# Spreading the last two batches' first norm over the fill of a quantised feed-forward

## What is computed

```python
x = x + xattn0(layernorm(x), ctx)      # softmax attention, 16 heads
x = x + ffn0(layernorm(x))             # quantised feed-forward
x = x + xattn1(layernorm(x), ctx)      # gated mLSTM attention, 8 heads
x = x + ffn1(layernorm(x))             # linear plus gated LoRA

def ffn0(x):                           # 256 -> 1024 -> 256
    h = layernorm(x) * ln1_g + ln1_b
    h = bitlinear(h, w1, b1)           # per-token 8-bit levels, ternary weights
    h = layernorm(gelu(h)) * ln2_g + ln2_b
    return bitlinear(h, w2, b2)
```

## Time and profile before

| | us |
|---|---|
| median of 3 runs | 406.5 (406.21 to 407.29) |
| time of the profiled execution | 406.27 |
| its span | 404.6 |
| busy: PE, DVE, ACT, POOL | 332.8, 305.9, 264.3, 183.8 |

### The profile page before, as it was taken

How to read it: one execution, slowest core, us unless ns; L and a number is a source line. 1 busy time by engine, 2 the same in 40 slices (tenths; PEclk the granted TensorE clock), 3 DMA queues, 4 the chain that set the end, 5 groups by cost and what they waited for, 6 DMA issues and landing times.

```text
span 404.6 us, 9204 instructions
## 1 busy us (share of the span) xinstructions
PE 332.8 (82%) x3118; PEld 235.1 (58%) x3118; DVE 305.9 (76%) x1025; ACT 264.3 (65%) x567; POOL 183.8 (45%) x207
## 2 busy tenths in 40 slices
PE   2989789999999999922667877869887999999975
PEld 1767567776777777611444555546455666666642
DVE  2799746777898989677899899897346787778772
ACT  1566444466545545734878988988667888888732
POOL 1213500211212375228999899885105545554550
PEclk9999999999999999965899999989999999999999
DMA  7699998969553440000000000000001212221101
GB/s 238 214 291 270 251 253 224 253 137 269 119 122 81 122 62 3 1 0 0 2 1 2 0 2 1 2 0 0 2 12 29 41 42 40 54 53 42 26 27 39
DMA packets 43869, 33.68 MB, mean 83 GB/s; under 512 B 19888, under 2 KB 39728, under 8 KB 43696
## 3 DMA queue, kind: packets, MB, share of 16 engines
q1 hardware_dynamic: 43824, 33.11, 32.9%
HBM read 24.71 MB, written 8.39 MB: 82 GB/s over the span
## 4 chain that ended last, share of the span: by engine, by line
PE 53%; DVE 19%; issue 14%; ACT 8%; POOL 5%; DMA 1%; SPq 0%; POOLq 0%; DVEq 0%; ACTq 0%
PE PS L1250 5%; PE PS L1169 5%; PE PS L1486 4%; PE PS L1239 4%; DVE sm L745 4%; PE PS L1308 4%; PE PS L1472 4%; PE PS L1230 4%; PE PS L1229 4%; PE PS L1269 3%; PE PS L1445 2%; PE PS L1467 2%; ACT pT L1000 2%; DVE sm L717 2%; PE PS L1435 2%
## 5 line engine op out<-in xcount | busy, mean ns | idle before, releaser
L1000 ACT ACTIVATE pT<-PS 128x512 f32<-128x512 f32 x64 | 36.5, 596 | 48.3 <-PE PS L1230 47.9
L610 DVE TENSOR_REDUCE negm<-PS 128x4 bf16<-128x512 f32 x64 | 42.3, 684 | 13.0 <-PE PS L1239 12.8
L439 POOL TENSOR_TENSOR sm<-sm,mhalf 128x1 f32<-128x1 f32 x16 | 11.3, 708 | 81.1 <-DVE sm L642 81.1
L455 POOL TENSOR_TENSOR kst<-kst,rows 128x1024 f32<-128x1024 f32 x16 | 37.6, 2352 | 6.4 <-ACT kst L1068 6.2
L1115 ACT ACTIVATE lnT<-PS,Atok 128x128 f32<-128x128 f32 x128 | 36.3, 369 | 2.0 <-DVE lnb L853 0.8
L1348 PE MATMUL PS<-identf,w2f 128*128 128x128 f32 x128 | 19.2, 298 | 21.4 <-ACT w2f L1057 21.3
L1230 PE MATMUL PS<-identb,negm 128*128 128x128 bf16 x256 | 34.9, 220 | 0.0
L469 POOL TENSOR_TENSOR kst<-kst,rows 128x1024 f32<-128x1024 f32 x14 | 33.1, 2363 | 0.0
L1250 PE MATMUL PS<-pT,vx 128*32 128x128 f32 x512 | 27.1, 285 | 5.2 <-ACT pT L1000 5.2
L1348 PEld LDWEIGHTS PS<-identf,w2f 128*128 128x128 f32 x128 | 15.1, 151 | 26.0 <-ACT w2f L1057 20.6
L494 POOL TENSOR_TENSOR rr<-ms,mhalf 128x8 f32<-128x8 f32 x16 | 26.4, 1647 | 1.9 <-DVE ms L935 1.9
(11 more groups left out here) (222 smaller groups left out, 979.1 us busy)
## 6 DMA issues: line engine op xcount, KB each, us to landing
scr_q<-qpart SPq DMA_DIRECT2D x8, 384.0 KB, 3.3
scr_k<-kpart SPq DMA_DIRECT2D x8, 384.0 KB, 4.5
X<-in_x SPq DMA_DIRECT2D x8, 256.0 KB, 4.6
CTXT<-in_ctxT SPq DMA_DIRECT2D x8, 256.0 KB, 5.1
vx<-in_ctx SPq DMA_DIRECT2D x16, 128.0 KB, 3.0
out<-rest SPq DMA_DIRECT2D x16, 128.0 KB, 1.7
rows<-in_rows SPq DMA_DIRECT2D x1, 1544.0 KB, 8.4
qst<-scr_q SPq DMA_DIRECT2D x8, 192.0 KB, 4.4
```

Of the source, the lines that this page charges most:

```text
L455: gp.tensor_tensor(n2[q.slot], n2[q.slot], ln2g, ALU.mult).then_inc(b_g2, 1)
L610: v.tensor_reduce(negm[f.slot % 2][:, 4 * hg:4 * hg + 4], PS[:, 2 + hg % 2, :].rearrange("p (h k) -> p h k", h=4), AX_X, ALU.max, negate=T ...
L1000: s.activation(pT[:, hg, :], PS[:, hg % 2, :], ACT.Exp, scale=float(DH0) ** -0.5).then_inc(a_e, 1)
```

## The change

The norm of batch 14 and that of batch 15 are taken apart and put into turns 3 to 6 of DVE; `hidden(1)` comes before them. POOL's powers and bias additions follow into turns 3 to 6. ACT's gelu table is loaded after the last exp of the attention, its normalising of batch 0 comes before gelu(1), and its two `level` instructions follow turns 4 and 7. PE turns the levels of batch 2 earlier and issues products that nobody reads after `up(2)` and `up(3)` (8 each) and after `columns(4)` (10), into bank 1. The zero that carries waits of the first norm goes into a column of its own.

```diff
@@ POOL
+            def spread1(d):
+                z = sm1[d.slot % 2]
+                pool.wait_ge(l_w, d.b + 1)
+                gp.tensor_tensor(z[:, 3:4], z[:, 2:3], mhalf[:, 0:1], ALU.pow).then_inc(l_r, 1)
+            def residual(d):
+                pool.wait_ge(l_c, d.b * 7 + 4)
+                gp.tensor_tensor(X[:, d.b, :], X[:, d.b, :], b2r, ALU.add).then_inc(l_xb, 1)
...
@@ POOL turn_b, between L455 and L464
+                if tau == 3:
+                    spread1(Turn(NB - 2, 2, 3))
@@ POOL, the fill
             turn_a(*peeled(NB, NB, 4, 4))
-            turn_b(2, *peeled(2, NB, 4, 9))
-            turn_a(*peeled(NB + 1, NB, 4, 4))
-            turn_a(*peeled(NB + 2, NB, 4, 4))
-            for tau in range(3, NB + 8):
+            for tau in range(2, NB + 8):
                 turn_b(tau, *peeled(tau, NB, 4, 9))
+                if tau == 4:
+                    residual(Turn(NB - 2, 2, 3))
+                    spread1(Turn(NB - 1, 3, 3))
+                elif tau == 6:
+                    residual(Turn(NB - 1, 3, 3))
@@ DVE turn_b, at hidden (L759)
-                if b:
+                if tau == 3:
+                    ln1_affine(before_last, late["centred"])
+                if b and b.b > 1:
                     hidden(b)
+                if tau == 3:
+                    ln1_unit(before_last)
+                elif tau == 4:
+                    late["stats"] = ln1_stats(last)
+                elif tau == 6:
+                    ln1_unit(last)
@@ DVE turn_b, behind spreads (L779)
+                if tau == 4:
+                    late["centred"] = ln1_centre(last, late["stats"])
+                elif tau == 5:
+                    ln1_affine(last, late["centred"])
 @@ DVE, the fill
-            normalise(last)
             for i in range(2):
                 v.memset(mv23[i][:], 1.0).then_inc(b_mv, 1)
+            normalise(last)
             dve.wait_ge(b_mv, 2)
             stats2(first, 1)
             spreads(first, None, 1)
-            ln1_scale(before_last, ln1_centre(before_last, ln1_stats(before_last)))
+            hidden(Turn(1, 1, 0))
             update(last)
-            centred = ln1_centre(last, ln1_stats(last))
-            turn_b(2, *peeled(2, NB, 4, 9))
-            ln1_scale(last, centred)
-            for tau in range(3, NB + 8):
+            late = {"centred": ln1_centre(before_last, ln1_stats(before_last))}
+            for tau in range(2, NB + 8):
                 turn_b(tau, *peeled(tau, NB, 4, 9))
@@ ACT, attention's turn_a
                     exp(3)
+                    if b.b == NB - 1:
+                        s.preload_act_table_set("gelu_and_others")
@@ ACT turn_b, L1062 to L1069
+                if p and p.b == 0:
+                    normed(p, tau)
                 if b:
                     gelu(b)
+                if p and p.b > 0:
+                    normed(p, tau)
@@ ACT, the fill
-            turn_b(2, *peeled(2, NB, 4, 9))
-            turn_a(*peeled(NB + 2, NB, 4, 5))
-            turn_b(3, *peeled(3, NB, 4, 9))
-            turn_a(*peeled(NB + 3, NB, 4, 5))
-            for tau in range(4, NB + 8):
+            for tau in range(2, NB + 8):
                 turn_b(tau, *peeled(tau, NB, 4, 9))
+                if tau == 4:
+                    turn_a(*peeled(NB + 2, NB, 4, 5))
+                elif tau == 7:
+                    turn_a(*peeled(NB + 3, NB, 4, 5))
@@ PE, attention's turn_a, behind the last batch's L1287
+                    if c.b == NB - 1:
+                        columns(Turn(2, 2, 0))
@@ PE, turn_b
-                if a:
+                if a and a.b > 2:
                     columns(a)
+                if a and a.b == 4:
+                    keep_busy(1, 10)
 ...
                 if a:
                     up(a)
+                    if a.b in (2, 3):
+                        keep_busy(1, 8)
```

More of the change, by code:

```diff
@@ L131, in build @@
         wscale = sb("wscale", [128, 2])
-        spare = sb("spare", [128, 2])
+        spare = sb("spare", [128, 3])
         st = [sb(f"st{i}", [128, 12]) for i in range(2)]
@@ L433, in scale_rows @@
                 gp.tensor_scalar(row, row, by, None, ALU.mult).then_inc(s_sr, 1)
+            def spread1(d):
[5 more added lines that the diff above has]
+                gp.tensor_tensor(X[:, d.b, :], X[:, d.b, :], b2r, ALU.add).then_inc(l_xb, 1)
             def turn_a(_f, _b, _c, d):
                 if d:
[L437 to L442, removed]
+                    spread1(d)
+                    residual(d)
                     if 9 <= d.b < 12:
@@ L632, in ln1_stats @@
                 done(dve, l_u, d, -1)
-                take_wait()
+                take_wait(2)
                 return cl.mark(v.bn_stats(z[:, 8:14], X[:, d.b, :]))
@@ L646, in ln1_centre, with ln1_affine @@
                                                       op0=ALU.subtract, op1=ALU.mult))
-            def ln1_scale(d, centred):
+            def ln1_affine(d, centred):
                 z = sm1[d.slot % 2]
@@ L656, in ln1_scale, with ln1_unit @@
                 dve.wait_ge(l_c, centred)
-                h1 = cl.mark(v.scalar_tensor_tensor(out=u1[d.b], in0=t1[:], scalar=z[:, 3:4], in1=ln1b,
-                                                    op0=ALU.mult, op1=ALU.add))
-                dve.wait_ge(l_c, h1)
+                cl.mark(v.scalar_tensor_tensor(out=u1[d.b], in0=t1[:], scalar=z[:, 3:4], in1=ln1b,
+                                               op0=ALU.mult, op1=ALU.add))
+            def ln1_unit(d):
+                z = sm1[d.slot % 2]
+                dve.wait_ge(l_c, d.b * 7 + 4)
                 top = cl.mark(v.tensor_reduce(z[:, 4:5], u1[d.b], AX_X, ALU.max, apply_absolute_value=True))
@@ L683, in turn_a @@
                 if d:
-                    ln1_scale(d, centred)
+                    ln1_affine(d, centred)
+                    ln1_unit(d)
                 if c and 6 <= c.b < 12:
@@ L1035, in gelu, with normed @@
                 s.activation(gl[b.slot], hb[b.slot], ACT.Gelu, scale=wmean[:, 0:1]).then_inc(b_gl, 1)
+            def normed(p, tau):
+                act.wait_ge(b_sh, tau - 1)
+                done(act, b_u2, p, -1)
+                s.activation(n2[p.slot], gl[p.slot], ACT.Identity, scale=rs23[tau % 2][:, 0:1],
+                             bias=sh23[tau % 2][:, 0:1]).then_inc(b_n2, 1)
             def turn_b(tau, a, b, p, _q, c, d, e, f, g):
@@ L1079, in _ @@
             turn_a(*peeled(NB + 1, NB, 4, 5))
-            turn_b(2, *peeled(2, NB, 4, 9))
-            turn_a(*peeled(NB + 2, NB, 4, 5))
-            turn_b(3, *peeled(3, NB, 4, 9))
-            turn_a(*peeled(NB + 3, NB, 4, 5))
-            for tau in range(4, NB + 8):
-                turn_b(tau, *peeled(tau, NB, 4, 9))
-                if tau == NB + 2:
+            for tau in range(2, NB + 8):
+                turn_b(tau, *peeled(tau, NB, 4, 9))
+                if tau == 4:
+                    turn_a(*peeled(NB + 2, NB, 4, 5))
+                elif tau == 7:
+                    turn_a(*peeled(NB + 3, NB, 4, 5))
+                elif tau == NB + 2:
                     s.preload_act_table_set("exp_and_others")
@@ L1312, in _, with keep_busy @@
             pipeline(pe, NB, 4, 3, turn_a, head=8, tail=False)
+            def keep_busy(bank, count):
+                for _ in range(count):
+                    t.matmul(PS[:, bank, :], identb[:], maskb[:].unsqueeze(1).to_broadcast([128, 4, 128]), start=True, stop=True)
             def turned(b):
@@ L1372, in _ @@
                 turn_b(*peeled(tau, NB, 4, 9))
-            def keep_busy(bank, count):
-                for _ in range(count):
-                    t.matmul(PS[:, bank, :], identb[:], maskb[:].unsqueeze(1).to_broadcast([128, 4, 128]), start=True, stop=True)
             turned(NB - 1).then_inc(g_tp, 1)
```

## The result

The changed kernel takes 401.51 us (median of 4 executions, 400.39 to 402.77); the kernel before, on the same chip, 406.89 (406.21 to 408.15): a ratio of 0.9865, 95% interval 0.9841 to 0.9888. The profiled execution of after took 400.94 us, with a span of 399.1 against 404.6.

A forecast was written before the change was run, and what follows sets the result against it. The prediction took the fill to be bound by a loop of waits from `hidden` to `hidden`, delayed by norms ahead of `hidden(1)`. Its steps bring `hidden(6)` 4.96 us earlier: 406.5 - 5.0 = 401.5 us, range 400.4 to 403.6.

The forecast's parts named there:

- the sum: Chain of steps through the fill: hidden(6) at 204.67 against 209.63, 4.96 us earlier, making the span 399.6.
- Table load and gelu(0): On ACT, the load moves behind the attention's last exp, so gelu(0) begins at 170.13, 1.13 us earlier.
- Rival 2: The early table load holds ACT longer than its row, 1.28 more: 402.8 us; chance 0.04.
- The wait of L667 for POOL: DVE's scaling of batch 14 waits for POOL's power, queued behind a product; costs 0.07 us.
- The turns: DVE's steps from hidden(1) at 173.20 to hidden(6) at 204.67, priced from rows of the earlier trace.
- The second added wait: POOL's power of batch 15 waits for its variance, batch 2's product queued behind; addition done 196.4, wanted 196.55, 0.15 to spare.
- The fall, taken as likely as not: PE's clock may fall to half between 177.5 and 180.5 us, where PE has nothing to do.
- some tenths: Cost of a clock fall ending among PE's unread products; bounds 0 and 3.4 us lost, 0 taken.
- The gain kept for the range: A clock fall at 271.0 us might vanish: bounded by 1.7 us, 1.1 kept for the range, not counted.
- Rivals 3 and 4: Half clock outlasting the fill, 407.9 or 410.9 us, chance 0.03; later stages not moving, 406.5 us, chance 0.04.
- Rival 3's price: A full turn with PE at half clock estimated at about 9 us instead of 5.97.
- The 0.39 that I took from the earlier trace: DVE's scaling step of batches 14 and 15, priced like L645 of the same shape at 0.39 us.

The follow-up runs named there:

- gelu_first: Changed kernel with gelu(1) put back ahead of the normalisation of batch 0 on ACT: 403.88 us, ratio 0.9942.
- no_products: Changed kernel without the 26 products that nobody reads: 400.97 us, ratio 0.9884.
- control: The changed kernel unaltered, run again as the common measure of the others: 401.81 us, ratio 0.9883.
- no_preload: Changed kernel with the gelu table load left right in front of gelu(0): 402.78 us, ratio 0.9916.
- spread_further: Changed kernel without products, gelu(0) ahead of ACT's copy of batch 1's levels, batch 15's norm in five places of turns 4 to 9: 403.85 us.
- combined: Changed kernel without products, gelu(1) first, POOL's power of batch 14 ahead of batch 0's product, batch 15's centring right behind its statistics: 403.5 us, ratio 0.9926.

## Why the prediction was right

It gave 401.5 us in 400.4 to 403.6, and the chain of `hidden` starts came out step by step: 173.20, 179.16, 185.13, 191.77, 198.13, 204.67 forecast; 172.90, 178.80, 184.76, 191.42, 197.77, 204.22 measured. That the median came out as 401.51 is luck to some 0.4 us: before measured 406.89 beside it, not 406.5, and the gain was 5.4, not 5.0. Of that gain 5.30 is the fill, where the sum had 4.96; the sum's steps are right to 0.1 each, but for the start. Point by point:

- **Table load and gelu(0).** Forecast 170.13, measured 169.80. 0.11 of it is an attention that ended earlier (`hidden(0)` 168.05, not 168.16); 0.14 of the rest is the step from the copy to gelu(0), which I took as 0.40 from the earlier trace rows: with no load between them it is 0.26 (169.54 to 169.80), and the copy's row of 0.37 overlaps gelu's. Rival 2 fell: the load's row ends at 168.63 and the next activation begins at 168.64.
- **Normalisation first.** The wait of L667 for POOL was forecast at 0.1; L667 starts 0.11 after the last spread ends (178.29), when the power ends at 178.37. gelu_first shows what the order on ACT buys, 1.1 us, which the sum had no separate term for.
- **The turns.** `hidden(1)` to `hidden(6)`: forecast 5.96, 5.97, 6.64, 6.36, 6.54; measured 5.90, 5.96, 6.66, 6.35, 6.45. The second added wait sits where it was put (POOL 0.85 for the variance, power at 189.61, forecast 189.9), and POOL's addition for batch 2 ends at 195.89, ahead of scale2 at 196.19, as forecast with little to spare.
- **Products and clock.** The fall, taken as likely as not, came at 179.6. Its cost was set at "some tenths" between 0 and 3.4: 0.01 in after (`hidden(3)` to `hidden(4)` 6.66, without products 6.65), 1.2 in control. Neither is some tenths, though both lie between the bounds, and one reason behind the guess is wrong: the text counts on the products to limit the cost of a fall, which "should end among them". It ended among the first eight in after, but in control only at 188.1, behind columns(4), among the ten; and without them nothing in the fill waits for PE at half clock (no_products). In the fill they only add risk; whether they spare a fall behind it can't be told from these runs (no_preload had one with them).
- **The tail.** The gain kept for the range, up to 1.7 us for a fall that might vanish, is nothing: after has no fall near 271 us, and the time behind `hidden(6)` is within 0.1 of before's. Rivals 3 and 4 fell with that. Rival 3's price, 3 us a turn, was too high: 6.8 us of half clock in full turns cost spread_further 1.7.
- **What no step had.** The places of the norm's steps with two SBUF inputs, which I priced only by length. In after three of the four begin beside a power of POOL or while it is idle, and the fourth, at 195.80, slips in at the end of an addition, 0.06 us ahead of the next product (195.86), which it lengthens. The 0.39 that I took from the earlier trace rows, from start to next start, held for that reason, and that was luck: nothing in the forecast looked at it. In combined, the same way of summing put the fill at 34.5 and it was 38.30.

## What to carry to other kernels

A software pipeline's fill is priced by following one repeated instruction from turn to turn: what stands ahead of it in program order, though its own inputs are ready, is the gain, and here the sum held to some tenths. Before work is moved into a "free" gap of VectorE, look at what GpSimd runs in that gap, and count the moved instruction with the rest of GpSimd's product if its two tensor inputs lie in SBUF, as the product's do. Filler products on TensorE are tested by leaving them out: a shorter half clock is worth nothing where no wait ends on TensorE.

## What the runs showed of the hardware

A VectorE instruction with both tensor inputs in SBUF, begun while GpSimd multiplies or adds over 128x1024, ended about 0.3 us after GpSimd's in all eight cases of these runs: 1.63 to 2.64 us instead of 0.48. One that began in the last 0.09 us of such an addition (195.80 in after) kept its 0.48. Where VectorE began 0.06 to 0.12 us first, GpSimd's took 2.58 or 2.63 instead of 2.35. Instructions with one SBUF input weren't touched: in after, the update of `X` (one operand in PSUM) took 0.48 inside the addition of 199.37 to 201.73, as in this row of DVE:

```profile
199.68 0.48 DVE L789 SCALAR_TENSOR_TENSOR X<-PS,sm,X 128x256 f32<-128x256 f32 x1
```

The Trainium skill ("SBUF — State Buffer", section "Who interferes with whom") states this: two SBUF inputs on VectorE contend with a GpSimd instruction that reads SBUF, and the one that is issued first holds the shared ports until it is done. These rows agree, with the sizes above. A power, which reads SBUF too, didn't hold VectorE for the length of its row: in after, L667 of batch 14 began 0.03 us after a power of 0.71 (178.37) and took 0.48.
